# Layer 0 attention: transposed probabilities and small products take turns in three accumulation banks, in place of two banks and one

## The chip, the cores and the metric

The kernel runs on one core of a Trainium2 chip. The metric is device time in microseconds (us) of one execution. The engines named here are PE (TensorE, matrix products and transposes), ACT (ScalarE), DVE (VectorE), POOL (GpSimd) and SP (SyncE, which issues most transfers). PE writes only to PS, the accumulation memory of 8 banks, each 128 partitions x 512 f32; ACT and DVE read it from there.

## The reference, cut to what matters

Four layers, each an attention part and a feed-forward part added to the residual. The change is in layer 0's attention: 8 sequences of 512 tokens, 16 heads of 8 columns, with relative position terms added to the scores.

```python
scores = jnp.einsum('bhqd,bhkd->bhqk', q, k) / scale
...
scores = scores + (c2p + p2c) / scale
probs = jax.nn.softmax(scores, axis=-1)
ctx = jnp.einsum('bhqk,bhkd->bhqd', probs, v)
...
out = ctx @ Wo + bo + hidden_states
```

Layers 1 to 3 follow and are not touched.

## The kernel before, in words

Layer 0 is a loop of 540 steps (`STEPS0`), written out by hand for each engine in a function of its own (`l0_pe`, `l0_ac`, `l0_dv`, `l0_po`, `l0_sp`); the engines meet only through semaphores. Each engine carries out its instructions in the order in which they are written. A step is one block of 128 query rows of one head: 4 steps make a head, 64 steps make a sequence (called a batch here). Below, u is the step and r = u mod 64 is the step within its batch.

What an engine does for block v:

- PE, step v: `scores(v)`, two transposing products (L581) and two products (L584) into bank v mod 3 (banks 0 to 2). It waits for DVE to be through with block v - 3 and for the head's transfer `rd`.
- DVE, step v + 1: `least(v)` (L207) adds a window read by `own_ends` and `own_middle` of POOL, finds the row's extreme and writes the block to `PB[v % 6]` in SBUF, semaphore `s_mx`.
- ACT, step v + 2: `exp(v)` (L167) on that block in place, semaphore `s_ex`.
- PE, step v + 5: `p_tr(v)`, four transposes (L339) of the block into one bank, semaphore `t_mm`.
- ACT, step v + 6: `p_out(v)` (L171) copies that bank to SBUF (`ptb`), semaphore `to_a`.
- PE, when r mod 16 is 7 or 11: `pv`, products of the transposed probabilities of four heads with V (L157, 16 records of 128x512 in the trace at each of these steps), into bank 5.

In most steps PE has other products too: `g_of` (L157, on even steps, into bank 6, drained by DVE's `g_out`), and the *small products* `small_mm` for the next or the last batch: q at r = 1, k at 3, far at 13, g0 at 22, mo at 29, sw at 31, v at 51. The order within a PE step is scores, `p_tr`, `g_of`, small products, `pv`. ACT drains q, k, far and g0 (`xf_out`, one step after, semaphore `m_ac`), DVE drains v, mo and sw (`v_out`, `mo_out`, `tail`, one step after, semaphore `m_dv`).

ACT has further work at some steps: splits of q, k and far into parts (`split_ac`, at r = 5, 8, 11, 14, 17, 20, in turns with POOL), and the layer norm of the last batch at r = 47 to 50 (four activations, L167 on 128x128), after which POOL's `tail` (three operations on 128x512) begins.

Banks before: 0 to 2 scores, 3 and 4 `p_tr` in turns, 5 `pv`, 6 `g_of`, 7 all small products. So `p_tr(v)` waits until `p_out(v - 2)` is done, and a small product waits until the one before it is drained (`emptied`, `number`). The functions `small_bank` and `bank` say which bank a small product takes and what it waits for.

Of the kernel before, what the change touches and what calls it, by code (L numbers as in the profile page):

```python
# [9 lines left out]
ALU = mybir.AluOpType  # L10
# [4 lines left out]
NBH = NB * NH  # L15
# [123 lines left out]
def bc(ap, shape):  # L139
    return ap.to_broadcast(shape)  # L140
# [11 lines left out]
def quarters(ap):  # L152
    return ap.rearrange("p (q c) -> p q c", q=4)
# [16 lines left out]
def copy(ac, out, in_):  # L170
    return ac.e.activation(out, in_, ACT.Copy, bias=0.0, scale=1.0)  # L171


def ts(en, out, in0, s1, s2, op0, op1=None):
    if op1 is None:
        return en.e.tensor_scalar(out, in0, s1, None, op0)  # L176
    return en.e.tensor_scalar(out, in0, s1, s2, op0, op1)


def tt(en, out, in0, in1, op):  # L180
    return en.e.tensor_tensor(out, in0, in1, op)  # L181


def stt(dv, out, in0, s, in1, op0, op1):
    return dv.e.scalar_tensor_tensor(out, in0, s, in1, op0, op1)  # L185
# [37 lines left out]
def newton3(dv, y, v, tmp):  # L223

    dv.step(stt(dv, y, tmp, -0.5, tmp, ALU.mult, ALU.mult))
    dv.settle()
    dv.step(stt(dv, y, y, 1.0, v, ALU.mult, ALU.mult))
    dv.settle()
    return stt(dv, y, y, 1.5, tmp, ALU.add, ALU.mult)


def program(nc, a, out):
    ctx = ExitStack()
    with ctx:
        def sem(name):
            return ctx.enter_context(nc.semaphore(name))

        def sb(name, shape):
            return ctx.enter_context(nc.sbuf_tensor(name, shape, F32))

        X = sb("X", [128, NT, 128])
# [11 lines left out]
        PS = ctx.enter_context(nc.psum_tensor("PS", [128, 8, 512], F32))  # L253
# [83 lines left out]
        def tr(pe, out, in_):  # L337
            k = in_.shape[0]
            return pe.e.transpose(out, in_, ident[0:k, 0:k])  # L339
# [4 lines left out]
        PTN = 6  # L344
        ptb = A0.take(PTN, 4, 512)
        wq, wk, wv, wo, sw = (A0.take(128) for _ in range(5))
# [29 lines left out]
        lnsc, lnb, bot = (XNf[:, in_xn + 640 + 128 * k:in_xn + 768 + 128 * k] for k in range(3))  # L376
# [7 lines left out]
        T1 = A0.take(4, 128)  # L384
# [8 lines left out]
        B_PV, B_G, B_M = 5, 6, 7  # L393

        FIRST = {"q": 2, "k": 3, "v": 7, "far": 4, "g0": 6}

        def small_bank(what, b):
            return PS[:, B_M if b else FIRST.get(what, B_M), :]

        def band_bank(n, x):  # L400
            return PS[:, 4 if n < 2 and x else B_G, :]
# [28 lines left out]
        s_mm, s_mx, s_ex, t_mm, to_a = (sem("l0_" + k) for k in ("s_mm", "s_mx", "s_ex", "t_mm", "to_a"))  # L430
# [3 lines left out]
        m_mm, m_ac, m_dv, sp_a, sp_p = (sem("l0_" + k) for k in ("m_mm", "m_ac", "m_dv", "sp_a", "sp_p"))  # L434
# [8 lines left out]
        STEPS0 = 4 * NBH + 28  # L443
# [12 lines left out]
        def small(u):  # L456

            b, r = divmod(u, 64)
            uses = []
            if b >= 1:  # L460
                uses += [(k, b - 1, 0) for k in ("mo", "sw") if ENDS[b][k] == r]
            if b + 1 < NB:
                uses += [(k, b + 1, 0) for k, at in AHEAD.items() if r == at]
            return uses
# [3 lines left out]
        number, emptied, n_ac, n_dv = {}, [], 0, 0  # L468
# [9 lines left out]
        def written(n):  # L478

            return 96 * min(n // 2 + 1, SLOTS // 2) + 48 * max(0, n // 2 + 1 - SLOTS // 2)  # L480

        def loaded(en, G):
            en.wait_ge(opl[G % OPN], 64 * (G // OPN + 1))

# [4 lines left out]
        def l0_pe(pe):  # L489
# [5 lines left out]

            def bank(use):
                what, b, _ = use
                i = number[use]
                if i >= 5:
                    pe.wait_ge(*emptied[i - 1])  # L500
                return small_bank(what, b)

            def small_mm(use):
                what, b, g = use
                ps = bank(use)
                if what in ("q", "k"):
                    ins = mm(pe, ps, wq if what == "q" else wk, XT[:, b * SEQ:b * SEQ + SEQ], True, True)
# [76 lines left out]
                return pe.e.matmul(out, lhsT, rhs, start=False, stop=stop, skip_group_check=True)  # L584

            def p_tr(v):
                T = PS[:, 3 + v % 2, :]
                pe.wait_ge(s_ex, v + 1)
                if v >= 2:
                    pe.wait_ge(to_a, v - 1)  # L590
                for jb in range(4):
                    ins = tr(pe, T[:, jb * 128:jb * 128 + 128], PB[v % PBN][:, jb * 128:jb * 128 + 128])
                ins.then_inc(t_mm, 1)
# [41 lines left out]
            for u in range(STEPS0):  # L635
                n, ib = divmod(u, 4)
# [14 lines left out]
        def l0_dv(dv):  # L651
# [124 lines left out]
            def mo_out(b):  # L776
                dv.wait_ge(m_mm, number["mo", b, 0] + 1)
                dv.wait_ge(ld_end, 4 * 16)
                tt(dv, T1, quarters(PS[:, B_M, :]), bc(bot.unsqueeze(1), [128, 4, 128]), ALU.add).then_inc(m_dv, 1)

            def tail(b, r):

                at, xs = ENDS[b + 1], slice(b * 4, b * 4 + 4)
                for q in range(4):
                    if r == at["stats"][q]:
                        dv.wait_ge(*emptied[number["mo", b, 0]])
                        dv.step(dv.e.bn_stats(lst[:, q, :], T1[:, q, :]))
                if r == at["var"]:
                    dv.settle()
                    for q in range(4):  # L790
                        ins = dv.e.bn_aggr(lmv[:, q, :], lst[:, q, :])
                    dv.step(ins)
                    dv.settle()
                    ts(dv, lv, lmv[:, :, 1], 1e-7, None, ALU.add).then_inc(tn_v, 1)
                if r == at["scale"]:
                    dv.wait_ge(tn_v, 2 * b + 1)
                    dv.wait_ge(tn_q, b + 1)
                    dv.step(newton3(dv, ly, lv, ltmp))
                    dv.settle()
                    stt(dv, loff, lmv[:, :, 0], -1.0, ly, ALU.mult, ALU.mult).then_inc(tn_v, 1)  # L800
                if r == at["sw"] + 1:
                    dv.wait_ge(m_mm, number["sw", b, 0] + 1)
                    tt(dv, X[:, xs, :], quarters(PS[:, B_M, :]), X[:, xs, :], ALU.add).then_inc(m_dv, 1)
                for q in range(4):
                    if r == at["last"][q]:
                        dv.wait_ge(t1_ok, b + 1)
                        dv.step(dv.e.bn_stats(nst4[:, q, :], X[:, 4 * b + q, :]))
                if r == at["lastvar"]:
                    dv.settle()
                    for q in range(4):  # L810
                        ins = dv.e.bn_aggr(NMV[:, 4 * b + q, :], nst4[:, q, :])
                    dv.step(ins)
# [8 lines left out]
            for u in range(STEPS0 + 1):  # L821
                n, ib = divmod(u, 4)
                b, r = divmod(u, 64)
# [16 lines left out]
        def l0_ac(ac):  # L840
# [50 lines left out]
            def p_out(v):  # L891
                n, ib = divmod(v, 4)
                ac.wait_ge(t_mm, v + 1)
                if n >= PTN:
                    ac.wait_ge(pv_mm, (n - PTN) // 4 + 1)
                elif n == 2:
                    for k in range(2):
                        ac.wait_ge(wr[k], written(SLOTS - 2 + k))
                copy(ac, ptb[:, n % PTN, :, ib * 128:ib * 128 + 128], quarters(PS[:, 3 + v % 2, :])).then_inc(to_a, 1)

            xf_out("q", 0)
            split_ac(0, 0, 0)
# [24 lines left out]
            for u in range(STEPS0 + 1):  # L927
                n, ib = divmod(u, 4)
                b, r = divmod(u, 64)
# [676 lines left out]
        def normed(v):  # L1606

            return (nd_po if v % 2 else nd_dv, v // 2 + 1)
# [6 lines left out]
        def l2_pe(pe, l3_step):  # L1615
# [36 lines left out]
            def p_tr(v):  # L1652
                T = PS[:, 3 + v % 2, :]
                pe.wait_ge(*normed(v))
                if v >= 2:
                    pe.wait_ge(lo2_dv, v - 1)
                for jb in range(4):
                    ins = tr(pe, T[:, jb * 128:jb * 128 + 128], PB2[v % 4][:, jb * 128:jb * 128 + 128])
                ins.then_inc(t2_mm, 1)
# [502 lines left out]
        def l3_pe(pe):  # L2162
# [55 lines left out]
            def p_tr(v):  # L2218
                T = PS[:, T_BANK[v % 2], :]
                if v % 4 == 1:  # L2220
                    pe.wait_ge(nd_po, NPO3 + v // 4 + 1)
                elif v % 4 == 3:
                    pe.wait_ge(nd3_ac, v // 4 + 1)
                else:
                    pe.wait_ge(nd3_dv, v // 2 + 1)
                if v < 2:
                    pe.wait_ge(lo2_dv, NV2)
                if v >= 2:
                    pe.wait_ge(lo3_dv, v - 1)
                for jb in range(4):  # L2230
                    ins = tr(pe, T[:, jb * 128:jb * 128 + 128], PB3[v % 4][:, jb * 128:jb * 128 + 128])
                ins.then_inc(t3_mm, 1)
# [441 lines left out]
        def co_pe(pe):  # L2674
# [10 lines left out]
            def p_tr(v):  # L2685
                T = PS[:, 4 + v % 2, :]
                pe.wait_ge(s3_ex, NV3 + v + 1)
# [281 lines left out]
```

## Time and profile before

| | us |
|---|---|
| median of 3 runs | 2027.25 (2024.81 to 2028.61) |
| the profiled execution | 2026.8 |
| its span, first to last instruction | 2025.0 |
| the stretch of layer 0's loop, 48.4 to 778.9 of the span | 730.5 |

The time of the profiled execution is 1.8 us more than its span and 0.45 us less than the median. Over the whole span PE is busy 92%, ACT 73%, DVE 76%, POOL 59%. The profile has a matmul end some time after the next has started, since they are pipelined; so idle time of PE is shown only where a pause outlasts that.

### The profile page before, as it was taken

How to read it: one execution, taken by the hardware profiler on the slowest of the kernel's cores; microseconds unless marked ns; L12 is line 12 of the kernel's file. 1: busy time of each engine (PE TensorE's matmuls, PEld its weight loads, DVE VectorE, ACT ScalarE, POOL GpSimd, SP SyncE). 2: the span in 40 equal slices, each digit the busy share in tenths (PEclk: the TensorE clock that was granted, in tenths of full speed). 3: DMA queues.
4: the chain of work that ended last, by engine and by line, in shares of the span. 5: the costliest groups of instructions: out<-in, count | busy, mean ns of one | idle time of the engine just before them, and what ended most of it. 6: DMA issues, size and time to landing. Idle time of an engine off the chain costs nothing.

```text
span 2025.0 us, 38764 instructions
## 1 busy us (share of the span) xinstructions
PE 1853.1 (92%) x13250; PEld 1445.8 (71%) x13250; DVE 1529.7 (76%) x3911; ACT 1469.6 (73%) x2939; POOL 1199.5 (59%) x1027
## 2 busy tenths in 40 slices
PE   4899999999999995879988999999999788889998
PEld 3677777767777773655776888888877566668797
DVE  7687887778787884473588889888889778754686
ACT  6688889888888884433566677777777677775675
POOL 3888889898888873374345555555556444447100
PEclk7899999999999997799999999999999999999999
DMA  6989898898888882001000000000010000012001
GB/s 185 297 272 303 270 291 270 279 286 272 285 275 286 269 268 101 16 0 41 1 6 1 1 1 1 1 1 1 1 33 1 1 1 1 1 47 81 9 1 42
DMA packets 146151, 228.02 MB, mean 113 GB/s; under 512 B 16870, under 2 KB 104294, under 8 KB 145446
## 3 DMA queue, kind: packets, MB, share of 16 engines
q1 hardware_dynamic: 145014, 220.57, 34.7%
q10 hardware_dynamic: 944, 4.98, 0.6%
q8 instruction: 108, 1.77, 0.4%
q14 instruction: 85, 0.70, 0.1%
HBM read 140.17 MB, written 85.33 MB: 111 GB/s over the span
## 4 chain that ended last, share of the span: by engine, by line
PE 43%; ACT 6%; DVE 6%; POOL 2%; issue 1%; DVEq 0%; ACTq 0%; POOLq 0%
PE PS L157 11%; PE PS L339 8%; PE PS L161 8%; PE PS L163 8%; PE PS L162 8%; ACT AR L167 3%; ACT L167 2%; DVE AR L185 1%; DVE DR L181 1%; ACT PT L171 1%; DVE PT L181 1%; POOL AR L176 1%; DVE AR L193 0%; POOL X L181 0%; DVE AR L176 0%
## 5 line engine op out<-in xcount | busy, mean ns | idle before, releaser
L339 PE MATMUL PS<-ident,AR 128*128 128x128 f32 x3812 | 581.0, 276 | 47.2 <-ACT AR L171 17.0
L339 PEld LDWEIGHTS PS<-ident,AR 128*128 128x128 f32 x3812 | 444.1, 142 | 151.9 <-issue 60.8
L167 ACT ACTIVATE AR<-AR 128x512 f32<-128x512 f32 (+3 forms) x680 | 458.0, 678 | 57.9 <-DVE AR L207 20.7
L157 PE MATMUL PS<-AR 128*9 128x512 f32 (+7 forms) x4014 | 459.1, 360 | 40.3 <-DVE AR L1389 13.8
L181 POOL TENSOR_TENSOR AR<-AR 128x512 f32<-128x512 f32 (+5 forms) x325 | 385.3, 1200 | 183.7 <-DVE AR L181 61.3
L171 ACT ACTIVATE AR<-PS 128x512 f32<-128x512 f32 (+1 forms) x588 | 344.9, 588 | 112.6 <-PE PS L339 77.5
L207 DVE CUSTOM_DVE_ANT_0 AR<-PS,AR 128x512 f32<-128x512 f32 x512 | 342.1, 678 | 100.4 <-PE PS L584 87.6
L176 POOL TENSOR_SCALAR AR<-AR 128x512 f32<-128x512 f32 (+1 forms) x146 | 255.4, 1750 | 264.7 <-DVE AR L1793 195.7
L167 ACT ACTIVATE AR<-PS,AR 128x512 f32<-128x512 f32 x512 | 346.6, 688 | 79.3 <-PE PS L157 40.6
L157 PEld LDWEIGHTS PS<-AR 128*9 128x9 f32 (+4 forms) x4014 | 284.3, 130 | 144.4 <-issue 94.8
L193 DVE TENSOR_REDUCE AR<-PS 128x1 f32<-128x512 f32 x384 | 263.7, 687 | 82.9 <-PE PS L163 76.5
L171 ACT ACTIVATE PT<-PS 128x512 fp32r<-128x512 f32 x320 | 191.4, 598 | 161.3 <-PE PS L339 127.0
L181 DVE TENSOR_TENSOR AR<-PS,AR 128x512 f32<-128x512 f32 (+2 forms) x289 | 202.3, 700 | 51.1 <-PE PS L157 41.6
L181 POOL TENSOR_TENSOR AR<-XN,AR 128x384 f32<-128x384 f32 (+1 forms) x170 | 194.8, 1146 | 60.5 <-DMA XN<-scr 35.7
L181 DVE TENSOR_TENSOR PT<-PS,PT 128x512 fp32r<-128x512 f32 x320 | 217.0, 678 | 8.5 <-ACT PT L171 8.5
L584 PE MATMUL PS<-AR 128*128 128x448 bf16 (+4 forms) x1088 | 208.6, 275 | 0.0
L181 POOL TENSOR_TENSOR AR<-AR,XN 128x512 f32<-128x512 f32 x144 | 155.0, 1076 | 9.0 <-ACT AR L167 6.9
L581 PE MATMUL PS<-ident,XN 128*128 128x128 f32 x680 | 134.4, 280 | 3.2 <-DMA XN<-scr 3.2
L161 PE MATMUL PS<-MH,XNr 128*128 128x512 f32 x256 | 122.5, 479 | 0.8 <-ACT AR L167 0.8
L584 PEld LDWEIGHTS PS<-AR 128*128 128x128 bf16 (+1 forms) x1088 | 110.7, 104 | 6.1
L581 PEld LDWEIGHTS PS<-ident,XN 128*128 128x128 f32 x680 | 76.1, 142 | 46.5 <-issue 34.5
L161 PE MATMUL PS<-PT,VW 128*128 128x512 f32 x256 | 102.1, 399 | 0.0
(180 smaller groups left out, 3029.3 us busy)
## 6 DMA issues: line engine op xcount, KB each, us to landing
XN<-scr SPq DMA_DIRECT2D x85, 768.0 KB, 5.6
scr<-AR SPq DMA_DIRECT2D x262, 128.0 KB, 3.1
AR<-scr SPq DMA_DIRECT2D x43, 768.0 KB, 5.8
scr<-AR SPq DMA_DIRECT2D x128, 256.0 KB, 2.7
AR<-qsc SPq DMA_DIRECT2D x96, 192.0 KB
qsc<-AR SPq DMA_DIRECT2D x16, 384.0 KB, 3.7
qsc<-AR SPq DMA_DIRECT2D x16, 256.0 KB, 3.5
AR<-in_wgu SPq DMA_DIRECT2D x16, 256.0 KB, 3.0
```

Of the source, the lines that this page charges most:

```text
L157: return pe.e.matmul(out, lhsT, rhs, start=start, stop=stop)
L161: pe.e.matmul(out, l[0], r[0], start=start, stop=False)
L162: pe.e.matmul(out, l[1], r[0], start=False, stop=False)
L167: return ac.e.activation(out, in_, func, bias=bias, scale=scale, accum_out=accum)
L171: return ac.e.activation(out, in_, ACT.Copy, bias=0.0, scale=1.0)
L176: return en.e.tensor_scalar(out, in0, s1, None, op0)
L181: return en.e.tensor_tensor(out, in0, in1, op)
L193: return dv.e.tensor_reduce(out, in_, AX.X, ALU.max, negate=True)
L207: return dv.e.tensor_tensor_reduce(out, in0, in1, -1.0, 3.0e38, ALU.add, ALU.min, least)
L339: return pe.e.transpose(out, in_, ident[0:k, 0:k])
L581: pe.e.matmul(out, lhsT, rhs, start=start, stop=start, is_transpose=True, skip_group_check=True)
L584: return pe.e.matmul(out, lhsT, rhs, start=False, stop=stop, skip_group_check=True)
```

## The change

All uses of a bank by `p_tr` and by small products inside the loop are listed in the order in which PE comes to them (`turns`). Use i takes bank 3, 4 or 7 by i mod 3 and waits until use i - 3 is drained: by `p_out` if it was a transposed block, by `xf_out` or DVE if it was a small product. The small products of the first batch, which come before the loop, keep their banks. No instruction of any engine is added, removed or moved; what changes are banks and the semaphore values for which PE waits. ACT, DVE, POOL and SP wait as before.

```diff
         def small_bank(what, b):
-            return PS[:, B_M if b else FIRST.get(what, B_M), :]
+            return turn_bank((what, b, 0)) if (what, b, 0) in turn_of else PS[:, FIRST[what], :]
...
+        turns = []
+        for u in range(STEPS0):
+            if 0 <= u - 5 < 4 * NBH:
+                turns.append(("p", u - 5, 0))
+            turns += small(u)
+        turn_of = {use: i for i, use in enumerate(turns)}
+        TURN_BANKS = (3, 4, 7)
+
+        def turn_bank(use):
+            return PS[:, TURN_BANKS[turn_of[use] % 3], :]
+
+        def turn(pe, use):
+            i = turn_of[use]
+            if i >= 3:
+                what, v, _ = turns[i - 3]
+                if what == "p":
+                    pe.wait_ge(to_a, v + 1)
+                else:
+                    pe.wait_ge(*emptied[number[turns[i - 3]]])
...
             def bank(use):
                 what, b, _ = use
-                i = number[use]
-                if i >= 5:
-                    pe.wait_ge(*emptied[i - 1])
+                if use in turn_of:
+                    turn(pe, use)
                 return small_bank(what, b)
...
             def p_tr(v):
-                T = PS[:, 3 + v % 2, :]
+                T = turn_bank(("p", v, 0))
                 pe.wait_ge(s_ex, v + 1)
-                if v >= 2:
-                    pe.wait_ge(to_a, v - 1)
+                turn(pe, ("p", v, 0))
```

PE's instructions around the small product g0 (u = 22, r = 22): before, with the semaphores that a row waits for. The first pair of rows is `p_tr`, then `g_of`, then g0, then the next step's scores and `p_tr`.

```order
L339 MATMUL PS<-ident,AR 128x128 [waits l0_to_a,l0_s_ex]
L339 MATMUL PS<-ident,AR 128x128 x3
L157 MATMUL PS<-AR 128x128 [waits l0_g_o]
L157 MATMUL PS<-AR 128x128 x3
L339 MATMUL PS<-ident,AR 128x128 [waits l0_m_ac]
L339 MATMUL PS<-ident,AR 128x128 x3
```

The same rows of the changed kernel:

```order
L339 MATMUL PS<-ident,AR 128x128 [waits l0_to_a,l0_s_ex]
L339 MATMUL PS<-ident,AR 128x128 x3
L157 MATMUL PS<-AR 128x128 [waits l0_g_o]
L157 MATMUL PS<-AR 128x128 x3
L339 MATMUL PS<-ident,AR 128x128 [waits l0_to_a]
L339 MATMUL PS<-ident,AR 128x128 x3
```

Nothing has moved. The wait of `p_tr` on `to_a` stands in both, for block 15 before and block 14 now (v = 17 here); g0 waits for `to_a` of block 15 now.

PE's instructions at step u = 54, three steps after the small product v, in the kernel before (scores, then `p_tr`):

```order
L581 MATMUL PS<-ident,XN 128x128 [waits l0_s_mx]
L581 MATMUL PS<-ident,XN 128x2x64
L584 MATMUL PS<-AR 128x320
L584 MATMUL PS<-AR 128x192
L339 MATMUL PS<-ident,AR 128x128 [waits l0_to_a,l0_s_ex]
```

and in the changed one:

```order
L600 MATMUL PS<-ident,XN 128x128 [waits l0_s_mx]
L600 MATMUL PS<-ident,XN 128x2x64
L603 MATMUL PS<-AR 128x320
L603 MATMUL PS<-AR 128x192
L339 MATMUL PS<-ident,AR 128x128 [waits l0_m_dv,l0_s_ex]
```

Here `p_tr` now follows a turn that the small product v had, so it waits for DVE's `v_out` in place of ACT's `p_out`. That is so 14 times (after v and after sw); 22 times it is ACT's drain of a small product (`l0_m_ac`).

## Rows read from the trace of the kernel before

**Rows 1.** Loop's window: busy PE, PEld, DVE, ACT, POOL (x), clock, DMA share, GB/s.

```profile
48.40:778.90 730.50, 700.95 (x6370) 527.71 (x6371) 567.55 (x1544) 625.95 (x1122) 619.97 (x577) 0.99 0.87 274
```

**Rows 2.** Waits of PE, 48 to 782 us: total us, times, longest us.

```profile
PE PS L339 <- ACT AR L171: 16.5, 42, 1.3
...
PE PS L581 <- DMA XN<-scr: 3.2, 1, 3.2
```

**Rows 3.** Timeline of PE, r = 17 to 23 of the fourth batch: start, length, instruction, count, idle before.

```profile
350.88 0.39 PE L581 MATMUL PS<-ident,XN 128*128 128x128 f32 x2
...
351.32 0.60 PE L339 MATMUL PS<-ident,AR 128*128 128x128 f32 x4
...
353.07 0.39 PE L581 MATMUL PS<-ident,XN 128*128 128x128 f32 x2
...
354.00 0.63 PE L339 MATMUL PS<-ident,AR 128*128 128x128 f32 x4 [0.32 <-ACT AR L171]
...
358.07 0.63 PE L339 MATMUL PS<-ident,AR 128*128 128x128 f32 x4 [0.80 <-ACT AR L171]
...
358.75 0.61 PE L339 MATMUL PS<-ident,AR 128*128 128x128 f32 x4
...
359.63 0.63 PE L339 MATMUL PS<-ident,AR 128*128 128x128 f32 x4
```

**Rows 4.** Timeline of ACT, r = 14 to 22 of the same batch.

```profile
347.83 0.60 ACT L171 ACTIVATE AR<-PS 128x512 f32<-128x512 f32 x1 [0.42 <-PE PS L157]
...
355.44 0.61 ACT L171 ACTIVATE AR<-PS 128x512 f32<-128x512 f32 x1
...
357.34 0.58 ACT L171 ACTIVATE AR<-PS 128x512 f32<-128x512 f32 x1
...
358.44 0.58 ACT L171 ACTIVATE AR<-PS 128x512 f32<-128x512 f32 x1
```

**Rows 5.** Timeline of PE, r = 6 and 7 of the same batch.

```profile
334.02 0.38 PE L581 MATMUL PS<-ident,XN 128*128 128x128 f32 x2
...
334.60 0.63 PE L339 MATMUL PS<-ident,AR 128*128 128x128 f32 x4
...
335.29 0.39 PE L581 MATMUL PS<-ident,XN 128*128 128x128 f32 x2
...
336.21 0.63 PE L339 MATMUL PS<-ident,AR 128*128 128x128 f32 x4 [0.32 <-ACT AR L171]
```

**Rows 6.** Timeline of PE, r = 50, 51 and 54 of the same batch.

```profile
398.92 0.63 PE L339 MATMUL PS<-ident,AR 128*128 128x128 f32 x4 [0.41 <-ACT AR L171]
...
400.40 0.63 PE L339 MATMUL PS<-ident,AR 128*128 128x128 f32 x4 [0.18 <-ACT AR L171]
400.86 1.06 PE L157 MATMUL PS<-AR,XT 128*128 128x128 f32 x8
...
404.17 0.60 PE L339 MATMUL PS<-ident,AR 128*128 128x128 f32 x4
```

**Rows 7.** Timeline of POOL, r = 51: its `tail` begins.

```profile
400.72 2.64 POOL L181 TENSOR_TENSOR AR<-AR,XN 128x512 f32<-128x512 f32 x2 [0.33 <-ACT AR L167]
```

**Rows 8.** Timeline of DVE, r = 52, 58 and 60 of the same batch.

```profile
401.95 0.69 DVE L181 TENSOR_TENSOR AR<-PS,AR 128x512 f32<-128x512 f32 x1 [0.85 <-PE PS L157]
...
410.30 0.69 DVE L207 CUSTOM_DVE_ANT_0 AR<-PS,AR 128x512 f32<-128x512 f32 x1 [0.49 <-POOL AR L181]
...
414.02 0.72 DVE L762 STREAM_TRANSPOSE XN<-PS 128x512 f32<-128x512 f32 x1 [0.42 <-PE PS L157]
```

**Rows 9.** Timeline of ACT, end of the loop.

```profile
771.51 0.75 ACT L167 ACTIVATE AR<-AR 128x512 f32<-128x512 f32 x1
773.12 0.60 ACT L171 ACTIVATE AR<-PS 128x512 f32<-128x512 f32 x1 [0.86 <-PE PS L339]
...
777.50 1.09 ACT L171 ACTIVATE AR<-PS 128x512 f32<-128x512 f32 x2
...
780.32 0.60 ACT L171 ACTIVATE AR<-PS 128x512 f32<-128x512 f32 x1 [0.32 <-PE PS L339]
```

More of the change, by code:

```diff
@@ L778, in mo_out @@
                 dv.wait_ge(ld_end, 4 * 16)
-                tt(dv, T1, quarters(PS[:, B_M, :]), bc(bot.unsqueeze(1), [128, 4, 128]), ALU.add).then_inc(m_dv, 1)
+                tt(dv, T1, quarters(small_bank("mo", b)), bc(bot.unsqueeze(1), [128, 4, 128]), ALU.add).then_inc(m_dv, 1)
             def tail(b, r):
@@ L802, in tail @@
                     dv.wait_ge(m_mm, number["sw", b, 0] + 1)
-                    tt(dv, X[:, xs, :], quarters(PS[:, B_M, :]), X[:, xs, :], ALU.add).then_inc(m_dv, 1)
+                    tt(dv, X[:, xs, :], quarters(small_bank("sw", b)), X[:, xs, :], ALU.add).then_inc(m_dv, 1)
                 for q in range(4):
@@ L898, in p_out @@
                         ac.wait_ge(wr[k], written(SLOTS - 2 + k))
-                copy(ac, ptb[:, n % PTN, :, ib * 128:ib * 128 + 128], quarters(PS[:, 3 + v % 2, :])).then_inc(to_a, 1)
+                copy(ac, ptb[:, n % PTN, :, ib * 128:ib * 128 + 128], quarters(turn_bank(("p", v, 0)))).then_inc(to_a, 1)
             xf_out("q", 0)
```

## The prediction

> **What bounds the kernel now.** I read the windows first. The loop of layer 0 takes 730.5 us of the 2025.0 us span, and in it PE is busy 701.0, ACT 626.0, POOL 620.0 and DVE 567.6 us, the DMA engines 0.87 of the time, at a granted clock of 0.99, the 2.4 GHz level [rows 1]. PE has the least idle time, so what PE waits for is what the loop can win. The waits of PE come next: 16.5 us in 42 pauses of the transposes (L339) on ACT's copies, and one wait for a transfer in 540 steps, 3.2 us [rows 2]. The 42 are `p_tr(v)` waiting for `p_out(v - 2)`, the wait that the change eases.
>
> That figure is short of the true one, because a pause is shown only beyond the modelled end of the matmul before. The timeline gives the rest. In an undisturbed step `p_tr` starts 351.32 - 350.88 = 0.44 us after its scores. At r = 19 it starts 354.00 - 353.07 = 0.93 us after, so PE stood 0.49 us, of which 0.32 is shown [rows 3]. At r = 6 the distance is 0.58 (0.14 lost, none shown) and at r = 7 0.92 (0.48 lost) [rows 5]. With some 0.16 us more for each of the 42, the pauses come to about 16.5 + 42 x 0.16 = 23 us, and more with those that are not shown. That is the most that the change could win, about 1.2% of the time.
>
> The pauses are not spread evenly. In the fourth batch, which I take for all, they stand at r = 6 and 7, at 18 to 22, at 50 and 51, and a small one at 58. These are the places where ACT has extra work (drains and splits at r = 2 to 23, the norm at 47 to 50). In the steps without `pv` PE needs about 1.0 us and ACT 1.09 for an exponential and a copy (358.44 - 357.34 = 1.10 [rows 4]); PE runs up against ACT there, until a `pv` holds PE long enough for ACT to catch up.
>
> **The change part by part.** No instruction is added, so there is nothing to pay for but waits.
>
> *The eased wait.* Where no small product came in the last three turns, `p_tr(v)` now waits for `p_out(v - 3)`: ACT's copy of one step earlier, 1.1 us sooner or more. In the two steps after a small product it still waits for `p_out(v - 2)`. No pause of the sample batch stands in such a step: those are r = 2 to 5, 14, 15, 23, 24, 30 to 33, 52 and 53.
>
> *A: r = 6 and 7.* 0.14 + 0.48 = 0.62 us are lost [rows 5], less than the 1.1 us of ease, so both pauses go. `pv` follows at r = 7 and ACT catches up, so nothing gives it back. Six batches (the second to the seventh) have it: 6 x 0.62 = 3.7 us.
>
> *B: r = 18 to 22.* Here ACT waits for PE last at 347.83 and then works without a pause [rows 4], so its copies come when they came. PE loses 0.49 at r = 19 and about 1.0 at r = 22 (0.80 shown + 0.16), with some 0.4 at 18 and 20. The `p_tr` at r = 22 no longer waits, since the copy that it needs now began at 355.44 and took 0.61. But g0, two instruction groups behind it, takes the next turn and waits for the very copy that `p_tr` waited for, begun at 357.34 [rows 4]. So g0 starts at 358.07 at the soonest, in place of 358.75: 0.68 us are won of 1.9 [rows 3]. Behind g0 on PE stand the next step's scores, `p_tr` and `pv`, for which DVE and ACT wait. The next `p_tr` (r = 23) stands behind g0 in the turns and keeps its old wait, on the copy begun at 358.44 and done at 359.02; the pauses show about 0.13 us from a copy's end to PE's start (357.34 + 0.58 to 358.07 is 0.15), so it can start at 359.16 at best in place of 359.63. That leaves 0.47 us for the batch. Then `pv` comes and ACT has slack. Seven batches: 7 x 0.47 = 3.3 us.
>
> *C: r = 46 to 64.* PE loses some 0.57 at r = 50 (0.41 shown) and 0.34 at r = 51 (0.18 shown) [rows 6]. The small product v at r = 51 now waits for the copy that `p_tr` of r = 51 waited for. So v starts at 400.40, in place of 400.86: 0.46 us won. Behind it stands a chain without `p_tr`: ACT's norm sets off POOL's `tail` at 400.72 [rows 7], POOL then works without a pause and DVE still waits for it at 410.30. DVE stands once more for PE at 414.02, 0.42 us, for the end of `pv` [rows 8]; from there to r = 64 it has no pause, and PE waits for DVE's `g_out` next. So however early PE is, only 0.42 us of it reach the next batch: 6 x 0.42 = 2.5 us.
>
> *D: the end.* After the last `pv` of the loop ACT stands 0.86 us for a `p_tr`. PE had it late because the `p_tr` before that `pv` waited for a copy; eased by one copy, `pv` is 1.1 us earlier. ACT goes on at 771.51 + 0.61 (its pace from an exponential to the copy, as in the rows around) = 772.12, in place of 773.12: 1.0 us. The last five copies then follow each other by 0.48, which puts the last at 777.50 + 4 x 0.48 = 779.42 in place of 780.32: 0.9 us [rows 9]. Sum 1.9.
>
> Sum: 3.7 + 3.3 + 2.5 + 1.9 = 11.4 us. Smaller pauses of the first and the last batch are left out. From the profiled execution, 2026.8 - 11.4 = 2015.4; the median of the runs lies 0.45 us above that execution, so about 2015.5.
>
> *The new waits.* The third turn after a small product waits for that product's drain. After k, far and g0 that is an ACT instruction of the step before the old `p_out`'s, so it comes sooner than the old wait. After v and sw it is DVE (14 waits). In the sample DVE's `v_out` runs from 401.95 to 402.64 [rows 8] and the `p_tr` that now waits for it started at 404.17 [rows 6]: 1.5 us to spare, 1.1 once PE comes 0.46 sooner. I cost it at nothing; without this cover each microsecond that DVE is later costs 14 us at most.
>
> **The rivals.** *All pauses go.* Against it stand B and C, where g0, v and DVE take the wait over. For it: a wait may be worth more than my sample says where ACT idles for PE. Then 23 us are won: 2004. The Trainium skill (Perfetto Trace Analysis, Optimization Strategy) takes consistent bubbles on the engine that should be saturated as a sign of too few buffers; by that rule alone the whole 23 us would go. The trace shows such bubbles at the same r in batch after batch, but shows as well that a second wait lies close behind them.
>
> *Nothing is won, because something else sets the pace.* The transfers of the bands are busy 0.87 of the loop [rows 1]; or POOL's and ACT's chain of C holds in each batch from start to end. If so, PE's pauses only move to another wait: 2027, less 2 at most for the end. Against it: PE stood for a transfer once [rows 2], and DVE and ACT both stand for PE between the chains (347.83, 414.02). The Trainium skill (Perfetto Trace Analysis, Identifying the Most-Contended Engine) says that matmul busy time is no good measure and that one should improve the engine with the highest occupancy; here that would be ACT or the transfers and the change would give nothing. The rows above bear that out only inside the stretches B and C.
>
> *Slower.* DVE's `v_out` or the addition after sw comes after `p_tr` wants the bank. It decides once DVE is more than 1.1 us later than in rows 8. At 2.5 us later, each of 14 waits costs 1.4 us, some 20 us, against 11 won: 2036. For it: DVE is behind by such an amount at r = 58, where it waits for POOL [rows 8]. Against it: `v_out` is written directly behind a `least` which PE's next scores need in any case.
>
> **How the numbers follow.** Chances: partial gain as summed 0.62 (own range 2007 to 2022), all pauses 0.14, nothing 0.19, slower 0.05. What a measurement of this kernel tells from no change is 0.2%, 4 us. The partial and the full case lie beyond 4 us, and of the nothing case 0.02 does: faster 0.78, same 0.17, slower 0.05. The range 2003 to 2025 takes in the full case's 2004 and the nothing case down from 2025; it leaves out less than 2 in 10. The likeliest is 2015.5.
>
> **What the profile after would show.** PE's pauses of the transposes on ACT's copies: from 42 to a handful at r = 6, 7, 18 to 20, 50 and 58. New pauses of about 1 us at g0 (r = 22), also on ACT's copies, and none on DVE at r = 34 and 54. The wait of `g_of` for DVE at r = 0 grows by 0.2 us or so. The loop's end is 11 us sooner; layers 1 to 3 take what they took. The prediction is wrong if the pauses go and the loop is not shorter (then transfers or POOL's chain set its pace, and PE's waits for `rd` or for `g_out` grow), or if the gain is above 18 us (then the second waits that I found do not hold).

## The result, and the profile after

| | before | after | ratio, 95% interval |
|---|---|---|---|
| median | 2027.93 us (4 runs, 2024.81 to 2028.62) | 2015.16 us (4 runs, 2013.18 to 2017.61) | 0.9943 [0.9928, 0.9959] |
| the same two kernels again | 2025.97 us (11 runs) | 2014.38 us (5 runs) | 0.9943 [0.9929, 0.9957] |

The change made the kernel 0.57% faster. The execution that was profiled took 2017.61 us, the slowest of the four; its span is 2015.8 us. The window of the loop, as in [rows 1]:

```profile
48.20:768.40 720.20, 694.81 (x6368) 530.06 (x6368) 564.28 (x1544) 625.39 (x1121) 619.99 (x577) 0.99 0.88 278
```

The loop is 10.3 us shorter (730.5 to 720.2) at the same clock, with the same work. Layers 1 to 3 took what they took: from the last transposes of the loop to the end there are 1245.3 us before (779.65 to 2024.98) and 1246.7 after (769.11 to 2015.78). The waits of PE in the loop of the changed kernel, in the columns of [rows 2] (L600 was L581):

```profile
PE PS L157 <- DVE AR L181: 11.7, 15, 1.8
PE PS L339 <- ACT AR L171: 8.7, 12, 1.6
PE PS L600 <- DMA XN<-scr: 2.4, 2, 1.4
PE PS L157 <- ACT AR L171: 1.3, 6, 0.2
```

The pauses on ACT's copies went from 42 to 12, none of the transposes waits for DVE, and a line of its own shows the new, small pauses of the small product v on a copy. The waits of products for DVE grew: before, that line was

```profile
PE PS L157 <- DVE AR L181: 8.6, 11, 1.6
```

PE at r = 18, 19, 22 and 23 of the fifth batch (the fourth, shown of before, was held up at r = 20 in this execution), beside [rows 3]:

```profile
440.13 0.38 PE L600 MATMUL PS<-ident,XN 128*128 128x128 f32 x2
...
440.57 0.60 PE L339 MATMUL PS<-ident,AR 128*128 128x128 f32 x4
...
441.23 0.39 PE L600 MATMUL PS<-ident,XN 128*128 128x128 f32 x2
...
441.67 0.63 PE L339 MATMUL PS<-ident,AR 128*128 128x128 f32 x4
...
444.57 0.63 PE L339 MATMUL PS<-ident,AR 128*128 128x128 f32 x4
445.03 0.39 PE L157 MATMUL PS<-AR 128*128 128x128 bf16 x4
446.09 0.66 PE L339 MATMUL PS<-ident,AR 128*128 128x128 f32 x4 [0.68 <-ACT AR L171]
446.58 0.38 PE L600 MATMUL PS<-ident,AR 128*128 128x128 f32 x2
...
447.28 0.63 PE L339 MATMUL PS<-ident,AR 128*128 128x128 f32 x4
```

The distance from the scores to `p_tr` is 0.44 us at r = 18 and 19: these pauses are gone. The pause has moved to g0 (446.09), and `p_tr` at r = 23 stands 447.28 - 446.58 - 0.44 = 0.26 us. ACT's copies for which the two wait, beside [rows 4]:

```profile
445.41 0.62 ACT L171 ACTIVATE AR<-PS 128x512 f32<-128x512 f32 x1
...
446.50 0.63 ACT L171 ACTIVATE AR<-PS 128x512 f32<-128x512 f32 x1
```

They end at 446.03 and 447.13, 0.06 and 0.15 us ahead of PE. At r = 6 and 7 of the same batch, beside [rows 5], both distances are 0.44:

```profile
423.05 0.38 PE L600 MATMUL PS<-ident,XN 128*128 128x128 f32 x2
...
423.49 0.60 PE L339 MATMUL PS<-ident,AR 128*128 128x128 f32 x4
...
424.15 0.39 PE L600 MATMUL PS<-ident,XN 128*128 128x128 f32 x2
...
424.59 0.64 PE L339 MATMUL PS<-ident,AR 128*128 128x128 f32 x4
```

At r = 51 and 54, beside [rows 6], v waits in place of `p_tr`, and `p_tr` of r = 54 starts 0.43 us after its scores, without a pause:

```profile
485.81 0.63 PE L339 MATMUL PS<-ident,AR 128*128 128x128 f32 x4
486.67 1.16 PE L157 MATMUL PS<-AR,XT 128*128 128x128 f32 x8 [0.22 <-ACT AR L171]
...
489.81 0.38 PE L600 MATMUL PS<-ident,XN 128*128 128x128 f32 x2
...
490.24 0.60 PE L339 MATMUL PS<-ident,AR 128*128 128x128 f32 x4
```

ACT at the loop's end no longer stands for PE, and its last copy ends at 770.43 in place of 780.92 [rows 9]:

```profile
767.22 0.78 ACT L167 ACTIVATE AR<-AR 128x512 f32<-128x512 f32 x1
767.83 2.60 ACT L171 ACTIVATE AR<-PS 128x512 f32<-128x512 f32 x5
```

To see where the time came from I took the start of each step's scores in both traces. The table gives by how much each stretch of steps became shorter (us; minus: longer). "Others" are the first and the last batch, the middle stretches, and the difference at the loop's start.

| stretch | term | predicted | first profile after | the same kernel again |
|---|---|---|---|---|
| r = 1 to 8, second to seventh batch | A | 3.7 | 3.5 | 3.5 |
| r = 16 to 24, first batch | B | 0.5 | -2.1 | 1.4 |
| r = 16 to 24, second to seventh batch | B | 2.8 | 2.1 | 2.5 |
| r = 49 to 64, second to seventh batch | C | 2.5 | 3.5 | 3.5 |
| r = 64 to 65, into the third to the last batch | C | 0 | -2.2 | -2.0 |
| r = 49 to the last transposes, last batch | D | 1.9 | 1.8 | 1.9 |
| r = 48 to 49, second to seventh batch | - | 0 | -0.8 | 0.5 |
| others | - | 0 | 4.8 | 3.4 |
| sum, before rounding | | 11.4 | 10.5 | 14.6 |

Both columns are taken against one execution before (2026.8 us). The executions profiled after took 2017.61 and 2009.48 us, so the last column shows the fastest of its five runs and has the larger sum. The two differ by 4.1 us at the loop's end, 2.3 of it by the end of the first batch: in the first profile PE stood there at r = 20 for a transfer that had landed in time in the other, and ACT stood 1.34 us for POOL at its split of r = 20, which it did not in the other.

```profile
82.97 0.41 PE L600 MATMUL PS<-ident,XN 128*128 128x128 f32 x2 [1.03 <-DMA XN<-scr]
```

### The profile page after: what moved, and what is told of

It is laid out like the page before. It is cut to its first block, busy times and chain, and to the rows that moved or that the text cites. A ratio compares the mean times of both kernels' runs of the same rounds, so it can differ in the third digit from the quotient of the medians.

```text
span 2015.8 us, 38764 instructions
## 1 busy us (share of the span) xinstructions
PE 1844.2 (91%) x13250; PEld 1445.2 (72%) x13250; DVE 1528.4 (76%) x3911; ACT 1469.0 (73%) x2939; POOL 1196.8 (59%) x1027
## 4 chain that ended last, share of the span: by engine, by line
PE 42%; DVE 7%; ACT 6%; POOL 2%; issue 2%; DVEq 0%; ACTq 0%; POOLq 0%
PE PS L157 10%; PE PS L339 8%; PE PS L161 8%; PE PS L163 8%; PE PS L162 8%; ACT AR L167 3%; ACT L167 2%; DVE AR L185 1%; DVE PT L181 1%; DVE DR L181 1%; POOL AR L176 1%; ACT PT L171 1%; DVE AR L181 1%; DVE AR L193 1%; POOL X L181 1%
## 5 line engine op out<-in xcount | busy, mean ns | idle before, releaser
L600 PE MATMUL PS<-ident,XN 128*128 128x128 f32 x680 | 134.5, 280 | 2.4 <-DMA XN<-scr 2.4
L600 PEld LDWEIGHTS PS<-ident,XN 128*128 128x128 f32 x680 | 76.0, 142 | 46.1 <-issue 31.8
```

Source lines behind the costliest of these rows:

```text
L600: pe.e.matmul(out, lhsT, rhs, start=start, stop=start, is_transpose=True, skip_group_check=True)
```

## The experiments

All edits are to the changed kernel, and every ratio is against the kernel before. My theory: the gain comes from the eased wait of `p_tr` at the steps named in A, B, C and D, and second waits close behind cap it in B and C. The rivals: the banks as such matter (not the waits), or the gain has another place.

**The old waits, in the new banks.** The three banks stay in turns, and the waits of before are added to the new ones.

```diff
             def bank(use):
                 what, b, _ = use
                 if use in turn_of:
                     turn(pe, use)
+                if number[use] >= 5:
+                    pe.wait_ge(*emptied[number[use] - 1])
                 return small_bank(what, b)
...
                 turn(pe, ("p", v, 0))
+                if v >= 2:
+                    pe.wait_ge(to_a, v - 1)
```

> The three banks in turns stay, but every transposition waits for the copy two blocks back as before, and every small product also for the small product before it. My theory (the gain is the eased wait alone; which bank is used costs or gives nothing): the time of the kernel before, 2027, within 3 us, with the pauses of the transposes on ACT's copies back at about 16.5 us in 42. Rival (the placing in banks itself changes the time): it stays near the changed kernel's 2015.

2027.48 us, ratio 1.0008 [0.9995, 1.0020]. Nothing is left of the gain: it comes from the waits. Both kinds are back here, those of `p_tr` and those of the small products; that it is the wait of `p_tr` I read from the trace of the kernel before, which shows no small product standing for a copy. Another execution, profiled for its trace:

> Three banks in turns with the old waits, for its trace alone: 16 to 17 us of the transposes waiting for ACT's copies in about 42 pauses, as in the kernel before, and the loop's end within 2 us of that one's 778.9.

It took 2028.1 us, and PE's waits for copies are back, nearly as before [rows 2]:

```profile
PE PS L339 <- ACT AR L171: 17.6, 43, 1.4
```

**One part at a time.** `p_tr` has the old wait too, but for the steps of A (the line below), of B (`16 <= (v + 5) % 64 <= 22`) or of C (`v < 443 and (v + 5) % 64 in (50, 51, 58)`).

```diff
+                if v >= 2 and not ((v + 5) % 64 in (6, 7)):
+                    pe.wait_ge(to_a, v - 1)
```

> The wait is eased only at steps 6 and 7 of each batch (term A, 0.62 us in each of six batches). By my sum 3.7 us less than before: 2023.5, with each batch shorter by 0.6 and no shift of the pauses elsewhere. Rival (the pause only moves to the wait of the small bands for DVE at the batch's first step, or to a transfer): 2027, with those waits grown by 0.6 each.

> The wait is eased only at steps 16 to 22 (term B). By my sum 0.47 us in each of seven batches, since g0 and the transposition behind it take the wait over: 3.3 us less than before, 2024, with a new pause of about 1 us at g0. If g0's turn did not hold, 1.9 us a batch and 2014. Rival (nothing is kept, the transfers set the pace): 2027.

> The wait is eased only at steps 50, 51 and 58 of the first seven batches (term C). By my sum 0.42 us in each of six batches, 2.5 us less than before: 2025. If DVE's and POOL's chain to the next batch's first step holds wholly: 2027 with the wait there grown by as much as was won. If it does not hold at all: 1.1 us in each of six batches, 2020.

| part | us | ratio | its own stretch: median of the second to the seventh batch, us | r = 64 to 65 |
|---|---|---|---|---|
| A | 2024.34 | 0.9992 [0.9982, 1.0003] | 0.65 (r = 1 to 8) | 0.0 |
| B | 2023.49 | 0.9997 [0.9984, 1.0009] | 0.48 (r = 16 to 24) | 0.0 |
| C | 2026.09 | 1.0004 [0.9991, 1.0017] | 0.03 (r = 49 to 64) | 0.0 |
| whole change | 2014.38 | 0.9943 [0.9929, 0.9957] | 0.65, 0.48, 0.53 | -0.5 |

No part alone can be told from no change by its time. By these times the three come to some 1.4 us together, give or take 4 (0.0008 + 0.0003 - 0.0004 of 2025 us); with 1.8 for D that is short of the 11.6 of the whole change. So the times do not show that the parts add up to the whole. Where each part wins is shown by the traces alone, and where the rest of the difference lies stays open. In the traces A and B win in their stretches what they win in the whole change, and leave the other two as they were, in the median. (B's trace is of another execution of it, 2019.99 us:)

> The wait eased only at steps 16 to 22, for its trace alone: of those steps' pauses only the one at g0 and 0.26 us at step 23 remain, and 0.47 us is won there in each batch.

C alone won nothing, since the pauses moved to later steps that kept their old wait. Counted from r = 49, it is as far ahead of the kernel before at r = 54 as the whole change, 0.29 us. PE in C alone, r = 54 of the fourth batch (scores, then `p_tr`):

```profile
400.42 0.38 PE L600 MATMUL PS<-ident,XN 128*128 128x128 f32 x2
...
401.04 0.63 PE L339 MATMUL PS<-ident,AR 128*128 128x128 f32 x4
```

That is 0.62 us, 0.18 more than undisturbed, where the kernel before had 404.17 - 403.73 = 0.44 [rows 6]. At r = 56 the rest of the 0.29 us is lost, and the 0.2 us that r = 58 wins are lost at r = 59, where `p_tr` stands as long as at r = 54. To list the steps with a pause is not to list the steps that need the ease.

**g0 three steps later.** If g0 in the turns limits B, it should be worth more to take it out of the stretch in which ACT is behind.

```diff
-        AHEAD = {"q": 1, "k": 3, "far": 13, "g0": 22, "v": 51}
-        XF_OUT = {2: "q", 4: "k", 14: "far", 23: "g0"}
+        AHEAD = {"q": 1, "k": 3, "far": 13, "g0": 25, "v": 51}
+        XF_OUT = {2: "q", 4: "k", 14: "far", 26: "g0"}
```

> The changed kernel with the small product g0 and its drain three steps later, at step 25 of a batch, behind the products with V, where ACT has slack; nothing else. If it is g0's turn that keeps term B at 0.47 us a batch, its pause of about 0.9 us and the one of the transposition behind it of 0.26 us go: 7 x 1.2 = 8 us less than the changed kernel, 2007. Rival (ACT's pace holds PE at the next wait all the same, or the corrections on POOL come late without g0): 2015, with the pause at another transposition, or at DVE.

2010.71 us, ratio 0.9929 [0.9915, 0.9942]. In the trace r = 16 to 24 won 1.58 us in place of 0.48, but 0.44 of it is g0's own time, which now stands behind r = 24. So 0.66 us more a batch, 4.6 us for seven, where 1.2 and 8 were expected: g0's pause is gone, but that of `p_tr` at r = 23, which was to go as well, grew from 0.26 to 0.49 us (0.93 after its scores). The edit also moves g0's copy on ACT, so it does not part g0's turn from that work. The time came out 3.7 us lower than that of the changed kernel in the same call (2014.38), and the intervals overlap.

**DVE's statistics a step later.** In the table the gain of r = 49 to 64 is lost at the next batch's first step, where `g_of` waits for DVE. I suspected four small operations at r = 62 (L829) ahead of it on DVE, and moved them behind.

```diff
-                  "norm": (47, 48, 49, 50), "sum": 51, "last": (58, 58, 60, 60), "lastvar": 62}] * NB
+                  "norm": (47, 48, 49, 50), "sum": 51, "last": (58, 58, 60, 60), "lastvar": 63}] * NB
```

> The changed kernel with DVE's four small statistics instructions (0.4 us) at step 63 in place of 62, so that they stand behind the addition for which PE waits at the next batch's first step. If DVE's chain from the end of the products with V sets that wait, the pause of 0.6 us there falls by 0.4 in each of six batches: 2.4 us less than the changed kernel, 2013. Rival (POOL's corrections set it): no change, 2015, with the same pause.

2014.68 us, ratio 0.9946 [0.9933, 0.9959]: nothing, a miss. The reason is in three timelines of DVE and POOL around r = 62. Before (DVE's product in `heads_out`, its `g_out`; POOL beside the product):

```profile
416.97 0.55 DVE L181 TENSOR_TENSOR AR<-XN,AR 128x128 f32<-128x128 f32 x1
...
418.05 0.68 DVE L181 TENSOR_TENSOR AR<-PS,AR 128x512 f32<-128x512 f32 x1
```

```profile
416.31 1.05 POOL L181 TENSOR_TENSOR AR<-AR 128x512 f32<-128x512 f32 x1
```

After, with DVE's transposition of r = 60 ahead of them:

```profile
411.08 0.72 DVE L780 STREAM_TRANSPOSE XN<-PS 128x512 f32<-128x512 f32 x1
...
414.03 0.85 DVE L181 TENSOR_TENSOR AR<-XN,AR 128x128 f32<-128x128 f32 x1
...
415.42 0.68 DVE L181 TENSOR_TENSOR AR<-PS,AR 128x512 f32<-128x512 f32 x1
```

```profile
413.69 1.05 POOL L181 TENSOR_TENSOR AR<-AR 128x512 f32<-128x512 f32 x1
```

PE after, `g_of` of r = 64:

```profile
416.25 0.38 PE L157 MATMUL PS<-AR 128*128 128x128 bf16 x4 [0.46 <-DVE AR L181]
```

And with the statistics behind, at the end of the second batch:

```profile
230.44 1.27 DVE L181 TENSOR_TENSOR AR<-XN,AR 128x128 f32<-128x128 f32 x1
```

```profile
230.49 1.07 POOL L181 TENSOR_TENSOR AR<-AR 128x512 f32<-128x512 f32 x1
```

The product takes 0.55, 0.85 and 1.27 us. It ends at 417.52, 414.88 and 231.71, each time 0.14 to 0.16 us after POOL's operation beside it (417.36, 414.74, 231.56). Whatever DVE gains ahead of the product, it stands longer in it. In two of the batches of this kernel, the fourth and the sixth, the product did not run into POOL's operation in that way and took 0.29 us; there the pause at the next batch's first step is gone. That is 1.1 us over the batches, too little for the time to tell.

**That product behind `g_out`.** Then POOL may hold it, and PE does not wait for it.

```diff
-                elif piece == 2:
+                elif piece == (3 if g == 2 else 2):
```

> The changed kernel with one DVE instruction (the 128x128 product of the heads' output with the reciprocal, two operands in SBUF) one step later for one head group in four, so that it stands behind the addition for which PE waits at the first step of a batch. It took 0.55, 0.85 and 1.27 us there in three kernels and ended each time within 0.2 us of the end of the POOL instruction beside it. If it is held by POOL and sets PE's pause of 0.6 us: the pause all but goes, 6 x 0.5 = 3 us less than the changed kernel, 0.9928 of the kernel before. Rival (POOL's corrections or the drain before it set the pause): 0.9943, the pause stays.

2014.89 us, ratio 0.9941 [0.9928, 0.9955]: a miss in the time. But the pause at the next batch's first step is gone, in each of the batches (r = 64 to 65: +0.1 in the median in place of -0.5). DVE, POOL and PE at the place shown above:

```profile
414.88 0.68 DVE L181 TENSOR_TENSOR AR<-PS,AR 128x512 f32<-128x512 f32 x1
415.48 1.03 DVE L181 TENSOR_TENSOR AR<-XN,AR 128x128 f32<-128x128 f32 x1
```

```profile
415.05 1.32 POOL L181 TENSOR_TENSOR AR<-XN,AR 128x512 f32<-128x512 f32 x1
```

```profile
416.02 0.39 PE L157 MATMUL PS<-AR 128*128 128x128 bf16 x4
```

So the product ahead of `g_out` was the cause of the wait, and 3.1 us came back over the batches. They went again: r = 1 to 8 won 0.7 us less in six batches, 48 to 49 lost 2.4 us in six batches in place of 0.8, and the third batch came out 1.0 us worse at 24 to 48 and as much at 49 to 64. The place is again DVE beside POOL, here in the third batch at r = 46 to 48 (DVE's four small operations, POOL ahead of and beside them, PE's `g_of`):

```profile
299.72 2.44 DVE L185 SCALAR_TENSOR_TENSOR AR<-AR 128x4 f32<-128x4 f32 x4
```

```profile
294.74 1.00 POOL L181 TENSOR_TENSOR AR<-XN,AR 128x384 f32<-128x384 f32 x1 [2.40 <-DMA XN<-scr]
...
300.89 1.05 POOL L181 TENSOR_TENSOR AR<-AR,XN 128x512 f32<-128x512 f32 x1
```

```profile
303.72 0.38 PE L157 MATMUL PS<-AR 128*128 128x128 bf16 x4 [2.75 <-DVE AR L181]
```

POOL had stood 2.40 us for a band's transfer, then worked without a pause up to 301.94, and DVE's four operations on 4 columns ended only at 302.16. In the kernel before, POOL stood 1.69 us for that transfer and the four took 1.67. How much of the loss at r = 48 is due to the transfers' own spread from one execution to the next I could not settle: this pause is 0.5 to 1.9 us in the changed kernel, batch by batch.

**Combinations.** g0 and the statistics later, g0 and the product later, and the changed kernel once more beside them:

> Both moves together: 2015 - 8 - 2.4 = about 2005, if the two waits are independent; if one only hides the other, as fast as the better one alone.

> The same with g0 three steps later as well: if the two waits are independent, 3 us less than with g0 later alone (0.9929), so 0.9914 of the kernel before; if one hides the other, 0.993.

> The changed kernel once more, on the same chip as the three beside it, so that they can be compared: 0.994 of the kernel before.

| | us | ratio |
|---|---|---|
| g0 and the statistics later | 2008.57 | 0.9926 [0.9911, 0.9942] |
| g0 and the product later | 2008.31 | 0.9917 [0.9904, 0.9929] |
| the changed kernel again | 2014.38 | 0.9943 [0.9929, 0.9957] |

The second has the lowest median, 0.83% under the kernel before, near the 0.9914 expected if the two waits are independent. Neither combination can be told from g0 later alone (0.9929), since the intervals overlap. In the second g0 has no pause any more, and what is left in r = 16 to 24 is one of `p_tr` at r = 23 on its third-last turn's copy, 353.51 - 352.59 - 0.44 = 0.48 us:

```profile
352.59 0.39 PE L600 MATMUL PS<-ident,XN 128*128 128x128 f32 x2
...
353.51 0.63 PE L339 MATMUL PS<-ident,AR 128*128 128x128 f32 x4 [0.32 <-ACT AR L171]
```

## Why the prediction was right, and where it was not

Forecast 2015.5 us, measured 2015.16; forecast gain 11.4 us, measured 12.8 and, the second time, 11.6.

*A* is right: 3.5 us measured for 3.7, and the part alone shows the same 0.65 us a batch and nothing given back at the next batch's first step. Its time alone (0.9992) does not show the gain.

*B* is right in its mechanism and size: g0 took the wait over, and the undisturbed batches won 0.48 us each for 0.47. With g0 and its copy moved the stretch won more, so g0's place was a cap, and the copy for `p_tr` at r = 23 is the next one. What failed is only to count seven undisturbed batches. In the first profile the first batch lost its lead to a transfer and to ACT's wait for POOL, and the fourth lost 0.9 us (0.4 in the second profile). There B's premise that ACT works without a pause did not hold. ACT's splits stood for POOL, the one of r = 14 for 0.72 us and the one of r = 20 for 0.69 (0.21 and 0.71 in the second profile), and g0 stood 1.48 us in place of 0.68:

```profile
354.21 0.63 ACT L171 ACTIVATE AR<-AR 128x512 bf16<-128x512 f32 x1 [0.69 <-POOL AR L181]
...
355.99 0.66 PE L339 MATMUL PS<-ident,AR 128*128 128x128 f32 x4 [1.48 <-ACT AR L171]
```

*C* is the term that was mis-sized: 2.5 us forecast, 1.3 measured (3.5 - 2.2), most of it at the border to the last batch. The step that failed is the overlap behind r = 60: "from there to r = 64 it has no pause", from which "only 0.42 us of it reach the next batch" was to follow. DVE has no pause there, but one of its operations is not of fixed length. DVE's transposition at r = 60 came 414.02 - 411.08 = 2.94 us earlier than before, `g_out` only 418.05 - 415.42 = 2.63, and the difference is the product's 0.85 - 0.55 = 0.30. At r = 49 that batch was 2.64 us ahead, so of C 0.30 us reached the transposition, in place of 0.42, and nothing was left at `g_out`.

POOL's operation beside the product came 416.31 - 413.69 = 2.62 us earlier, as early as the batch was at r = 49. From its `tail` to there POOL works without a pause in both traces, and the `tail`, which waits for ACT's norm, began 400.72 - 398.07 = 2.65 us earlier [rows 7]:

```profile
398.07 2.67 POOL L181 TENSOR_TENSOR AR<-AR,XN 128x512 f32<-128x512 f32 x2 [0.33 <-ACT AR L167]
```

So what PE wins at r = 50 and 51 does not move POOL, and POOL's time reaches `g_out` through the product. The rival that POOL's and ACT's chain holds the batch from start to end had this right.

That the product's place ahead of `g_out` makes the wait is shown, by the kernel that moves it. That POOL holds it is read from the ends of the two, which go together in four kernels (the fourth: 416.51 and 416.37); I did not move POOL's operation. The loop has 32 such products, and all of them in the kernel before agree. The 14 with no POOL operation beside them took 0.28 or 0.29 us. One, of 0.29 us too, began 0.09 us before the end of a POOL operation. Each of the other 17 took longer, 0.41 to 1.15 us, and ended 0.14 or 0.15 us after the end of a POOL operation. The Trainium skill (SBUF — State Buffer, Who interferes with whom) says that a DVE instruction with two inputs in SBUF contends with a GpSimd instruction that reads SBUF, through a pair of ports that it calls an exclusive lock. The trace agrees, with 0.14 to 0.16 us from POOL's end to the product's. So the product could not be costed by its length before.

*D* is right: 1.8 us for 1.9.

*The new waits* cost nothing, as said: PE never waited for DVE in `p_tr`, and `v_out` (487.87 to 488.56 in the fifth batch) was done 1.7 us ahead of the `p_tr` that waits for it (490.24):

```profile
487.87 0.69 DVE L181 TENSOR_TENSOR AR<-PS,AR 128x512 f32<-128x512 f32 x1 [0.59 <-PE PS L157]
```

*What was left out* is what made the sum come true. The first and the last batch won 4.0 us in the first profile outside the terms (2.7 and 1.3), against the losses of B and C and 0.8 us at r = 48. So the hit to 0.3 us is partly luck.

*The rivals.* All pauses go: no, 12 are left of 42, those at g0 above all, and second waits took over, as argued. Nothing is won: no for A, B and D; for C it was so at five of six borders, but for 0.3 us or less, through POOL and DVE. Slower: the two waits on DVE never ended last.

## What to carry to other kernels

Where two users of a shared set of buffers take turns, the pause moves to the next user in the turns; to size the gain, follow the second wait down the queue to the point where the other engine catches up, and count only what arrives there. An operation on an engine that runs without a pause need not be one of fixed length, since a neighbouring engine can stretch it (0.28 to 1.15 us here): look at the spread of its length over the trace before taking "no pause" as "comes earlier by the same". Where the gain per place is under the noise of the time, read starts of one instruction step by step in two traces: gains of 0.5 us in a stretch agreed to 0.02 here, in the batches that nothing else disturbed.

## What the runs showed of the hardware

One DVE product of 128x128 took 0.28 us where POOL was idle beside it (below, of the third batch at r = 46 in the kernel with the product later), and 0.55, 0.85, 1.03 and 1.27 where POOL had an operation under way. In the longest of these DVE's row starts 0.05 us ahead of POOL's (230.44 and 230.49), while POOL's operation before it had not ended, and it was still DVE that ended after the whole of the next one. It is not always so: in the changed kernel a product that began at 253.44, 0.13 us before the end of one POOL operation and 0.09 before the start of the next, took 0.29. In all fourteen traces no such product with POOL idle beside it took 0.30 us or more, and each that took 0.30 or more ended 0.14 to 0.16 us after a POOL operation. Four DVE operations on 4 columns took 2.44 us beside POOL working without a pause.

```profile
302.08 0.28 DVE L181 TENSOR_TENSOR AR<-XN,AR 128x128 f32<-128x128 f32 x1
```
